# Second self attention of a two-layer decoder: score products issued for two heads into two banks, and one mask product for each bank

## What is computed

```python
q = x @ Wq; k = x @ Wk; v = x @ Wv             # 16 heads of 4, 4 key heads of 4, 4 value heads of 8
s = q @ k.T * scale + slope[h] * (j - i)       # for every head h, 256 queries i, 256 keys j
s = where(j <= i, s, -inf)
out = softmax(s) @ v                           # then a projection and the residual
```

## Time and profile before

| | |
|---|---|
| time, median of 3 runs | 623.69 us (620.76 to 624.16) |
| the profiled execution's own time | 619.47 us |
| its span from first to last instruction | 617.5 us |
| PE busy | 529.0 us, 86% of the span |
| DVE busy | 424.6 us, 69% |
| ACT busy | 323.5 us, 52% |
| mean granted clock of PE | 0.954 |

### The profile page before, as it was taken

The page is one execution under the profiler, slowest core; times in us unless marked ns, Lnnn a source line. Parts: engine busy times, 40 slices in busy tenths (PEclk is TensorE's granted clock), DMA queues, the critical chain, the costliest instruction groups (busy, mean ns, idle before and its releaser), DMA issues. The chain is left out here.

```text
span 617.5 us, 12861 instructions
## 1 busy us (share of the span) xinstructions
PE 529.0 (86%) x4880; PEld 327.9 (53%) x4890; DVE 424.6 (69%) x1037; ACT 323.5 (52%) x807; POOL 192.1 (31%) x288
## 2 busy tenths in 40 slices
PE   2668787999999999778986489978988999999894
PEld 1433343344555656446554355766666867655453
DVE  6885764654463654798779876847557577889994
ACT  1423445567576674695733536554666555362440
POOL 3743200043245443432620031001113122435653
PEclk9965999999999999989997889999999999999998
DMA  8700000000030000000256005300000000303001
GB/s 299 267 1 2 2 2 3 1 3 2 1 136 3 1 1 1 2 2 1 80 143 243 3 17 156 97 11 3 4 2 2 3 3 1 138 2 137 2 1 34
DMA packets 25815, 27.92 MB, mean 45 GB/s; under 512 B 18177, under 2 KB 22794, under 8 KB 24858
## 3 DMA queue, kind: packets, MB, share of 16 engines
q1 hardware_dynamic: 25754, 27.10, 13.1%
HBM read 22.14 MB, written 4.75 MB: 44 GB/s over the span
## 5 line engine op out<-in xcount | busy, mean ns | idle before, releaser
L811 POOL TENSOR_TENSOR A_l0x_prob<-A_l0x_prob,A_l0x_inverted_sums 128x256 f32<-128x256 f32 (+1 forms) x32 | 25.9, 829 | 56.6 <-DVE A_l0x_inverted_sums L922 56.6
L811 POOL TENSOR_TENSOR B_l0x_prob<-B_l0x_prob,B_l0x_inverted_sums 128x256 f32<-128x256 f32 (+1 forms) x32 | 26.5, 848 | 45.1 <-DVE B_l0x_inverted_sums L922 45.1
L2080 PE MATMUL B_banks<-B_moe_xT,w_moe_rows 128*128 128x512 f32 x72 | 33.8, 596 | 1.7 <-DVE B_moe_h L2047 1.7
L2080 PE MATMUL A_banks<-A_moe_xT,w_moe_rows 128*128 128x512 f32 x72 | 34.3, 597 | 0.0
L324 DVE TENSOR_REDUCE B_l0a_nmax<-B_banks 128x2 f32<-128x512 f32 x32 | 21.4, 688 | 15.2 <-PE B_banks L226 11.9
L905 DVE TENSOR_REDUCE A_l0x_nmax<-A_banks 128x2 f32<-128x256 f32 (+1 forms) x32 | 16.3, 552 | 22.6 <-PE A_banks L980 22.5
L358 ACT ACTIVATE A_l0a_expT<-A_banks 128x512 f32<-128x512 f32 x32 | 18.3, 599 | 22.0 <-PE A_banks L310 22.0
L829 ACT ACTIVATE B_l0x_prob<-B_banks,B_l0x_nmax 128x128 f32<-128x128 f32 x64 | 26.0, 420 | 5.9 <-DVE B_l0x_nmax L905 5.7
L324 DVE TENSOR_REDUCE A_l0a_nmax<-A_banks 128x2 f32<-128x512 f32 x32 | 21.3, 688 | 9.8 <-PE A_banks L226 8.0
L829 ACT ACTIVATE A_l0x_prob<-A_banks,A_l0x_nmax 128x128 f32<-128x128 f32 x64 | 26.1, 425 | 1.7 <-DVE A_l0x_nmax L905 1.7
L846 ACT ACTIVATE A_l0x_probT<-A_banks 128x384 f32<-128x384 f32 x32 | 15.8, 493 | 19.3 <-PE A_banks L992 19.1
(11 more groups left out here) (609 smaller groups left out, 1570.7 us busy)
## 6 DMA issues: line engine op xcount, KB each, us to landing
w_toeplitz_rows<-in_toeplitz_rows SPq DMA_DIRECT2D x1, 3072.0 KB, 15.3
w_moe_rows<-in_moe_rows SPq DMA_DIRECT2D x1, 2304.0 KB, 9.6
w_l1x_rows<-in_l1x_rows SPq DMA_DIRECT2D x1, 2048.0 KB, 7.8
A_l1x_values<-A_l1a_v_tokens SPq DMA_DIRECT2D x4, 512.0 KB, 3.5
A_l1x_v_groups<-A_l1x_values SPq DMA_DIRECT2D x16, 128.0 KB, 3.1
B_l1x_values<-B_l1a_v_tokens SPq DMA_DIRECT2D x4, 512.0 KB, 3.5
B_l1x_v_groups<-B_l1x_values SPq DMA_DIRECT2D x16, 128.0 KB, 3.1
w_l0x_vo_rows<-in_l0x_vo_rows SPq DMA_DIRECT2D x1, 1024.0 KB, 9.0
```

Of the source, the lines that this page charges most:

```text
L811: ins = pool.tensor_tensor(pair, pair, bcast(rz[:, g % 2, i, :], 2, n), ALU.mult)
L2080: pe.matmul(hidden_bank(k)[:, :], w["moe_w3" if which else "moe_w1"][:, ORDER[i], part, :], xT[:], start=True, stop=True).then_inc(s_h.sem, 1)
```

## The change

The separate tensor_E goes; l1a now calls tensor_S_pair for the jobs of b = 0 and tensor_E_pair for all units, at every second turn. The turn of an odd head remains and issues no E. A pair waits until both banks are free, writes products of the two banks in turn, then one mask product for each bank. The mask's operand is the same 128 columns read n times over (n is 2 or 4), and the output is n blocks of a bank. The jobs of b = 1 keep tensor_S, with the merged mask. The jobs are in a new order, so that both of a pair have one shape: for each eight heads four of c = 1 and then two of c = 0. TURNS is written anew for all five engines, with the same number of turns of each lane.

```diff
-        self.jobs = [job for h in range(0, H, 4) for job in ((1, h, 2), (1, h + 2, 2), (0, h, 4))] if causal else [(None, h, 1) for h in range(H)]
+        self.jobs = [job for h in range(0, H, 8) for job in [(1, h + i, 2) for i in range(0, 8, 2)] + [(0, h, 4), (0, h + 4, 4)]] if causal else [(None, h, 1) for h in range(H)]
...
-            for i in range(n):
-                ins = pe.matmul(bank[:, (i + 1) * keys - P:(i + 1) * keys], self.w["ident_bf"][:], self.w["mask_q"][:], start=False,
-                                stop=True, skip_group_check=True)
+        if self.causal:
+            ins = self.masked(pe, bank[:, :].rearrange("p (h k) -> p h k", h=n)[:, :, 512 // n - P:512 // n], self.w["mask_q"])
...
-    def tensor_E(self, pe, u):
-        b, h = divmod(u, H)
-        bank = self.exp_bank(u)
-        if h == 0:
-            pe.wait_ge(*self.s_q(16 * self.G * (b + 1)))
-        if u >= 2:
-            pe.wait_ge(*self.s_p(u - 1))
...
+    def masked(self, pe, out, mask):
+
+        n = out.shape[1]
+        return pe.matmul(out, self.w["ident_bf"][:], mask[:].unsqueeze(1).broadcast_to([P, n, P]), start=False, stop=True, skip_group_check=True)
+
+    def score_products(self, m):
+
+        b, at = divmod(m, self.JOBS)
+        c, h, n = self.jobs[at]
+        if c is None:
+            return [(b, h, i * P, S, i * S) for i in range(SB)]
+        keys = (c + 1) * P
+        return [(b, h + i, c * P, keys, i * keys) for i in range(n)]
+
     def tensor_S_pair(self, pe, m):
 
         if m:
             pe.wait_ge(*self.s_mx(m))
...
+        first, second = self.score_products(m), self.score_products(m + 1)
+        if self.causal and len(second) == 4:
+            second = second[2:] + second[:2]
+        for i in range(len(first)):
+            for job, products in ((m, first), (m + 1, second)):
+                b, h, t, keys, at = products[i]
+                ins = pe.matmul(self.score_bank(job)[:, at:at + keys], self.q(b, h, t, P), self.k(b, h, 0, keys),
+                                start=(i == 0), stop=not self.causal, skip_group_check=True)
+                if i == len(first) - 1 and not self.causal:
                     ins.then_inc(self.s_s.sem, 1)
+        if self.causal:
+            for job in (m, m + 1):
+                _, h, n = self.jobs[job]
+                blocks = self.score_bank(job)[:, :].rearrange("p (h k) -> p h k", h=n)[:, :, 512 // n - P:512 // n]
+                self.masked(pe, blocks, self.w["mask_q"]).then_inc(self.s_s.sem, 1)
 
     def tensor_E_pair(self, pe, u):
 
...
         if u:
             pe.wait_ge(*self.s_p(u))
         for c in range(SB):
+            skipped = P if self.causal and c else 0
             for i in range(2):
...
+        if self.causal:
+            for i in range(2):
+                blocks = self.exp_bank(u + i)[:, :].rearrange("p (c k) -> p c k", c=SB)[:, :, 0:P]
+                self.masked(pe, blocks, self.w["mask_k"]).then_inc(self.s_e.sem, 1)
...
-            a.tensor_S(pe, u)
+            if u % 2 == 0:
+                a.tensor_S_pair(pe, u)
...
-            if n < U:
-                a.tensor_E(pe, n)
+            if n < U and n % 2 == 0:
+                a.tensor_E_pair(pe, n)
...
     "sync":
-        "W3 A1 W10 B1 A2 B2 L1 A6 L1 A3 B5 A1 B5 A2 B2 A1 B1",
+        "W2 A1 W11 B1 A2 B2 L1 A6 L1 A3 B5 A1 B5 A2 B2 A1 B1",
```

More of the change, by code:

```diff
@@ L223, in tensor_S @@
             pe.wait_ge(*self.s_mx(m - 1))
-        if c is None:
-            for c in range(SB):
-                ins = pe.matmul(bank[:, c * S:(c + 1) * S], self.q(b, h, c * P, P), self.k(b, h, 0, S),
-                                start=(c == 0), stop=True, skip_group_check=True)
-        else:
-            keys = (c + 1) * P
-            for i in range(n):
-                pe.matmul(bank[:, i * keys:(i + 1) * keys], self.q(b, h + i, c * P, P), self.k(b, h + i, 0, keys),
-                          start=(i == 0), stop=False, skip_group_check=True)
-            for i in range(n):
-                ins = pe.matmul(bank[:, (i + 1) * keys - P:(i + 1) * keys], self.w["ident_bf"][:], self.w["mask_q"][:], start=False,
-                                stop=True, skip_group_check=True)
+        products = self.score_products(m)
+        for i, (b, h, t, keys, at) in enumerate(products):
+            ins = pe.matmul(bank[:, at:at + keys], self.q(b, h, t, P), self.k(b, h, 0, keys), start=(i == 0), stop=not self.causal, skip_group_check=True)
+        if self.causal:
+            ins = self.masked(pe, bank[:, :].rearrange("p (h k) -> p h k", h=n)[:, :, 512 // n - P:512 // n], self.w["mask_q"])
         ins.then_inc(self.s_s.sem, 1)
@@ L252, in sync_shift @@
             sp.dma_start(dst, src).then_inc(self.s_q.sem, 16)
-    def tensor_E(self, pe, u):
-        b, h = divmod(u, H)
-        bank = self.exp_bank(u)
-        if h == 0:
-            pe.wait_ge(*self.s_q(16 * self.G * (b + 1)))
-        if u >= 2:
-            pe.wait_ge(*self.s_p(u - 1))
-        second = P if self.causal else 0
-        pe.matmul(bank[:, 0:S], self.k(b, h, 0, P), self.q(b, h, 0, S), start=True, stop=not self.causal, skip_group_check=True)
-        ins = pe.matmul(bank[:, S:self.W], self.k(b, h, P, P), self.q(b, h, second, S - second), start=False, stop=not self.causal, skip_group_check=True)
-        if self.causal:
-            for c in (0, S):
-                ins = pe.matmul(bank[:, c:c + P], self.w["ident_bf"][:], self.w["mask_k"][:], start=False, stop=True, skip_group_check=True)
-        ins.then_inc(self.s_e.sem, 1)
     def tensor_PV(self, pe, g, s_fin):
@@ L293, in tensor_S_pair @@
             pe.wait_ge(*self.s_mx(m))
-        for c in range(SB):
-            for h in (m, m + 1):
-                ins = pe.matmul(self.score_bank(h)[:, c * S:(c + 1) * S], self.q(0, h, c * P, P), self.k(0, h, 0, S),
-                                start=(c == 0), stop=True, skip_group_check=True)
-                if c == SB - 1:
-                    ins.then_inc(self.s_s.sem, 1)
+        first, second = self.score_products(m), self.score_products(m + 1)
[7 more added lines that the diff above has]
+                if i == len(first) - 1 and not self.causal:
+                    ins.then_inc(self.s_s.sem, 1)
+        if self.causal:
[3 more added lines that the diff above has]
+                self.masked(pe, blocks, self.w["mask_q"]).then_inc(self.s_s.sem, 1)
     def tensor_E_pair(self, pe, u):
@@ L2384 @@
     "tensor":
[8 rows of a table removed]
[L2393 removed]
[9 rows of a table removed]
[L2403 removed]
[5 rows of a table removed]
[8 rows of a table added]
+    "vector":
[9 rows of a table added]
+    "scalar":
[5 rows of a table added]
     "gpsimd":
[L2410 to L2411 removed]
+        "A12 B1 A3 B2 A1 B13 A11 B1 A2 B2 A1 B2 A2 B1 A1 B1 A1 B1 A2 B1 A1 B2 A2 B1 A1 B6 A1 B2 A1 B1 A3 B2 A2 B8 A8 B2 A2 B2 A1 B3 A2 B1 A1 B3 A1 B1 A1 B1 A1 "
+        "B1 A6 B1 A4 B3 A1 B3 A1 B7 A1 B1 A1 B2",
     "sync":
[L2413 removed]
+        "W2 A1 W11 B1 A2 B2 L1 A6 L1 A3 B5 A1 B5 A2 B2 A1 B1",
 }
```

8 lines of the change are left out of this document (3 added, 5 removed), and 44 rows, old and new, of the table TURNS.

## The result

The changed kernel takes 629.89 us (median of 4 runs, 629.41 to 631.49); the kernel before took 623.33 us beside it. The ratio is 1.0125, 95% interval 1.0098 to 1.0151 (it is estimated from all runs, and the quotient of the two medians is 1.0105): some 7 us slower, where the forecast was 1.1 and its own range ended at 627.5 (the range with the rivals, 618.8 to 630.5, holds it). The time is near the slower rival's 628.5 us, but by luck: the place and the mechanism are mostly not that rival's.

What follows compares the result with a forecast made beforehand. PE and DVE were taken to bound different stretches: DVE A's first pass, both B's, little slack in moe. Terms -0.4 + 1.8 + 0 - 0.3 = +1.1 us on 623.69 gave 624.8 us; range 622 to 627.5, with rivals 618.8 to 630.5.

Steps and rivals of the forecast that it cites:

- slower rival: B's first-pass gap arrives whole at moe, with A's 2 to 3 us: some 628.5 us; chance 0.27.
- part 4: Order lists of all engines: A's earlier context load gains 0.3 us, at most 0.9; shifted turns and job order 0.
- part 3: Second pass of l1a in pairs: longer round trip hidden beside other PE work, 0, between -3.5 and +2 us.
- part 2: First pass of l1a in pairs: B +2.6, A +1.0 us; half reaches the end, +1.8, between 0 and 6.
- Merged masks: Mask products in l1a: 144 fewer at 3 ns each, -0.4 us at most, 0 if PE is not the bound.
- slow output: Merged masks in l1a: two-block output costs its columns twice, up to 10.3 us more PE, some 631 us; chance 0.05.
- B's first pass: In l1a: five gaps of 0.81 or 0.92 us between pairs on DVE, +2.6 us, between 2.4 and 3.0.
- A's first pass: In l1a: gaps of about 6 us, fillable by B's ffn work if so ordered: +1.0 us, between 0 and 3.
- Second pass in pairs: In l1a: pair's longer round trip lies beside 1.3 us or more of other PE work, costing 0.
- Half of the delay is made up by 506 us: After the first passes, PE's 10.97 us idle from 409 to 506 us absorbs half, leaving +1.8 us.
- Order lists: Earlier context load for A at the start saves 0.3 us; turns shifted elsewhere keep the lanes level, 0.
- the new lists alone: Rival: the rewritten lists move the stages by more than the change, either way by 4 us; chance 0.05.

Runs made afterwards that it cites:

- e1: Kernel before with all new order lists, its code unchanged: 633.95 us, 1.0164 to the kernel before.
- e9: Kernel before with its old lists and single jobs and units, only the masks of a bank merged into one product: 622.54 us, 1.0000.
- e17: Kernel before with old lists, merged masks and the new job order, every job and unit in its own turn: 621.59 us, 0.9994.
- e2: Changed kernel's code with all old order lists: 636.56 us, 1.0221 to the kernel before.
- e10: Changed code on old lists, a pair's two jobs or units issued together at the even turn, each with its own wait and mask: 627.89 us, 1.0095.
- e3: Changed code on old lists with only the first pass in pairs, second-pass units one by one: 629.63 us, 1.0109 to the kernel before.
- e18: e17 with two second-pass units issued at the even head's turn, each with its own wait: 626.08 us, 1.0071 to the kernel before.
- e14: Changed code with new lists only from some 305 to 409 us (middle), old ones elsewhere: 630.30 us, 1.0123 to the kernel before.
- e8: Changed kernel with its new lists, a pair's two jobs or units issued one after the other with separate waits: 629.10 us, 1.0112.
- e5: Changed code with old lists up to some 305 us (head), new ones from there: 628.41 us, 1.0115 to the kernel before.
- e13: Changed code with new lists until some 409 us and old ones behind (tail): 634.30 us, 1.0189 to the kernel before.
- e7: Changed kernel with a separate product for each mask block, 144 more products: 632.41 us, 1.0156 to the kernel before.
- e15: e14 with a pair's two jobs or units issued one behind the other, a wait each: 629.40 us, 1.0114 to the kernel before.

## Why the prediction was wrong

The step that failed is in part 4: "The shifted turns elsewhere leave the lanes level to within a few turns, and I enter 0". With it fell the 0 of part 3 and the half of part 2 that was to be made up. The runs show that the new lists are worth 10 to 11 us by themselves (e1), and that in the changed kernel A's l1x is where it loses: 3.4 us to its first exponential, because 90 products of B and not 48 stand there, and 1.5 us before A's moe, in every profile with the new tail and in none without. Point by point:

- **Merged masks, -0.4: right** within what can be measured (e9: 1.0000, 144 products fewer). The slow output has fallen: 0.11 us for 256 columns in two blocks. The Trainium skill ("PSUM — Partial Sum Buffer", Specifications) says that any non-contiguous access pattern slows matmuls significantly. The trace disagrees for blocks of 128 columns; the bound taken for that case was +10.3 us of PE.
- **B's first pass, +2.6: right** (12.6 us for 10.3, and for 10.1 in e17), and the gaps of 0.81 and 0.92 us to 0.01. That the whole growth is the pair's is shown under the old lists only (13.0 us in e2, 10.5 in e10); under the new ones single jobs take 12.5 us too (e1).
- **A's first pass, +1.0: right for the new lists, wrong as a property of the code.** With the stage ahead of it, it went from 46.4 to 47.1 us (47.3 in e17). The condition, "if the written order puts it there", was the one that mattered: under the old lists the pass is 4 to 5 us longer (e3, e2), beyond the bound of 3.
- **Second pass in pairs, 0: wrong under the old lists,** where the early turn alone costs 0.7% (e18 over e17, some 4 us). I had named what stands behind the pair's wait and that it comes a turn earlier, and then priced only the round trip beside "1.3 us or more of other PE work". That cover is a mean over the loop, and PE waits at the few turns where it is thin: 4 waits for exponentials, 2.1 us, and longer waits at maxima and normalizings behind them. What the early turn costs under the new lists was not measured apart.
- **Half of the delay is made up by 506 us: wrong, and for another reason than its rival gives.** Against e17, A comes to its l1x input at the same time, so for A's lane nothing was left to make up. B's last exponential of l1a starts 2.1 us later (464.2 for 462.1), which is its first pass less what its loop gained. The delay that reaches the moe, 4.8 us for the first activation of A there, arises behind 430 us, in A's l1x. The idle time of PE in that stretch is not a reserve: PE waits there for maxima, exponentials and normalizings of the same two lanes. From 430.4 us to A's first l1x exponential PE is busy almost throughout, and what decides is whose products the list puts first.
- **Order lists, -0.3: wrong in kind.** They were entered as a small edit. The middle is worth -1.0% to the new code (e14 over e2) and +1.2% to the old, more than every term of the sum. The rival "the new lists alone, either way by 4 us, 0.05" named it and was too small in both: alone they cost 10 to 11 us.

The slower rival was 1.4 us from the end with 628.5 us, by luck: its mechanism, B's first pass arriving whole, is 2.1 us on B's lane at 464 us, and A's lane, which it wanted 2 to 3 us late, is not late until its l1x.

What stays open is whether any lists would carry the new code without loss. Under the new tail it pays in A's l1x, under the old one in A's second pass, and no list between was tried. Single exchanges from the changed kernel did not help clearly: not separate waits (e8), not the head (e5), not the tail (e13), not split masks (e7). Since the prices don't add up, this is no proof that each of them is innocent. The early turns of the odd jobs and units were not tried apart under the new lists, nor was the job order.

## What to carry to other kernels

Where the order of the engines' work is written out by hand, price a change under the lists that it comes with and not by the code alone: exchange code and lists once each, before anything else, because each half can cost more than the whole. Where lists are joined in the middle, look up for each engine at what time its join falls: equal counts of turns are not equal times.

Cut each lane into legs between events that every profile has, and put the legs of all runs side by side, sorted by list and by code. A leg that is longer under one list whatever the code shows where that list costs, which no window at fixed times shows.

Issuing two units in one turn is free only if the bank of the second is free at the place where the first stands, every time, not on average; look at the shortest distance between them in the timeline, not at the loop's mean. Two banks that are filled together and emptied together make their two engines take turns. It costs the full round trip of each pair unless other work of the waiting engine stands in exactly that gap.

Before idle time of an engine in a later stretch is counted on to take up a delay, read what ends that idle time: here it was mostly the same two lanes.

## What the runs showed of the hardware

- The granted clock fell to 1.2 GHz at 416 us after 2 us in which PE was busy for 0.61, with 1.51 of 2 before them, and stayed there until 420 us although PE was then busy without a gap. In the profiles of e5, e7, e13, e14 and e15 it fell near the same place too; in those of before, e2, e8 and e17 it did not. Here it took 1.7 us of full clock from PE, without making B's loop longer.
- A product whose output lies in two blocks of 128 columns with a stride, and one in four blocks (512 columns), cost their columns. The view of the mask's products by form, after:

```profile
L271 PE MATMUL A_banks<-w_mask_k,w_ident_bf x32: 272/273/421, 358.1 to 413.4; 128*128 128x256 bf16 x32
...
L271 PE MATMUL B_banks<-w_mask_q,w_ident_bf x24: 272/273/421, 397.3 to 436.6; 128*128 128x256 bf16 x16, 128*128 128x512 bf16 x8
```

  Their median duration is 273 ns for 256 columns, where the plain product of L262 took 0.27 us. Of the form with four blocks two start within 401.98 - 401.52 = 0.46 us in B's first pass, 0.23 each:

```profile
401.52 0.59 PE L271 MATMUL B_banks<-w_mask_q,w_ident_bf 128*128 128x512 bf16 x2
401.98 0.44 PE L1624 MATMUL A_banks<-w_const_rows,A_l1a_v_tokens 128*128 128x128 f32 x2
```

- Executions of equal instructions and lists differ by 3 us within the first 160 us. The fourteen kernels with the old head issue the same up to some 300 us, and B's last exponential of l0x starts between 300.5 and 305.2 us in their profiles. The lengths of later stages mostly agree to a few tenths (32.3 to 32.6 us nine times for the second line of the first table). That is why no reading above rests on a point in time of one profile alone.
